# A graph kernel's adjacency, cast and turned by DMA instead of by TensorE, with maxima over two segments at once

## The reference

```python
# layer 0: maximum over the neighbours, 0 for a row without any
masked = jnp.where(mask[:, :, None], x[None, :, :], neg)
out = jnp.where(has_nbr[:, None], jnp.max(masked, axis=1), 0)
x = _layernorm(x + out)
# layer 1: attention over the neighbours
h = x @ W
e = leaky_relu((h @ a_src)[:, None] + (h @ a_dst)[None, :], 0.2)
att = softmax(jnp.where(valid, e, -1e9), axis=1)         # valid: adj > 0
attention = jnp.where(att >= 1e-4, att, 0) * L[:, None]  # L: neighbours of the row
x = _layernorm(x + elu(h + attention @ h))
```

## Time and profile before

| | us |
|---|---|
| median of 3 runs | 1084.57 (1081.44 to 1092.72) |
| the profiled execution, its own time | 1078.43 |
| its span | 1076.5 |
| PE, DVE, ACT, POOL busy | 779.5, 675.2, 609.9, 272.1 |
| DMA | 169.08 MB, mean 157 GB/s |

### The profile page before, as it was taken

One profiled execution on the slowest core, in us unless ns is written; L12 is line 12 of the kernel. 1 busy time (PEld: TensorE's weight loads), 2 busy tenths in 40 slices (PEclk: granted clock), 3 DMA queues, 4 the chain that ended last, 5 costly groups with the idle time before them and its releaser, 6 DMA issues.

```text
span 1076.5 us, 16405 instructions
## 1 busy us (share of the span) xinstructions
PE 779.5 (72%) x5872; PEld 595.6 (55%) x5935; DVE 675.2 (63%) x1662; ACT 609.9 (57%) x1257; POOL 272.1 (25%) x275
## 2 busy tenths in 40 slices
PE   1698976957968959659779320399989899998615
PEld 0365644634635636436446120298889888888314
DVE  6558577557666766656675812648667766865371
ACT  1886663834835726526537100557977977885413
POOL 7100732713705607407417274000000000000000
PEclk9999998989979989979989655599999999999757
DMA  9287796894985976956977525531442354151200
GB/s 331 88 268 238 218 187 209 232 210 137 268 208 157 235 209 194 187 188 203 195 235 189 49 67 30 182 122 35 173 168 73 123 181 143 40 181 36 90 0 5
DMA packets 69154, 169.08 MB, mean 157 GB/s; under 512 B 7311, under 2 KB 27920, under 8 KB 68912
## 3 DMA queue, kind: packets, MB, share of 16 engines
q1 hardware_dynamic: 60672, 148.98, 40.4%
q0 software_dynamic: 8400, 19.02, 16.3%
HBM read 129.11 MB, written 40.96 MB: 158 GB/s over the span
## 4 chain that ended last, share of the span: by engine, by line
PE 42%; DVE 27%; DMA 13%; issue 9%; ACT 6%; POOL 3%; DVEq 0%; POOLq 0%
DMA adj_in<-in_adj_dram 12%; PE psS L900 11%; PE psT L1049 7%; DVE adj_in L1490 7%; PE psT L875 7%; PE psR L1049 6%; ACT adj_in L768 3%; PE psR L884 2%; DVE acc L1227 2%; POOL G L621 1%; DVE ident L1171 1%; DVE wide L1327 1%; PE psR L1115 1%; DVE listed L1323 1%; PE psS L945 1%
## 5 line engine op out<-in xcount | busy, mean ns | idle before, releaser
L684 ACT ACTIVATE at<-psT 126x512 bf16<-126x512 int32 (+1 forms) x264 | 157.4, 597 | 222.3 <-PE psT L875 221.7
L1227 DVE TENSOR_TENSOR acc<-acc,psS 128x512 f32<-128x512 f32 x248 | 168.9, 684 | 170.9 <-PE psS L900 170.2
L900 PE MATMUL psS<-hot,x_split 128*128 128x512 bf16 x774 | 224.0, 395 | 39.9 <-DVE acc L1227 23.6
L875 PE MATMUL psT<-ident,adj_in 128*126 128x128 f32 (+1 forms) x1056 | 177.0, 293 | 44.2 <-DMA adj_in<-in_adj_dram 44.2
L621 POOL DMA_INDIRECT G<-x_tab_dram,idx x128 | 121.3, 948 | 334.5 <-DVE y L1390 231.6
L1490 DVE SCALAR_TENSOR_TENSOR adj_in<-adj_in,at 128x3072 f32<-128x3072 f32 (+1 forms) x48 | 148.3, 3090 | 70.6 <-ACT adj_in L768 70.6
L768 ACT ACTIVATE adj_in<-acc,minus,r_col 128x512 f32<-128x512 f32 x264 | 189.3, 803 | 2.5 <-PE psT L1049 2.5
L692 ACT ACTIVATE hot<-psR 128x512 bf16<-128x512 f32 x264 | 156.3, 592 | 0.2 <-PE psR L884 0.2
L875 PEld LDWEIGHTS psT<-ident,adj_in 128*126 128x126 f32 (+1 forms) x1056 | 121.5, 148 | 50.2 <-DMA adj_in<-in_adj_dram 44.7
L1049 PE MATMUL psT<-h_seg,adj_in 128*128 128x130 f32 x1056 | 126.3, 281 | 21.0 <-DVE adj_in L1490 20.6
L900 PEld LDWEIGHTS psS<-hot,x_split 128*128 128x128 bf16 x792 | 75.5, 100 | 118.8 <-DVE acc L1227 32.1
(11 more groups left out here) (272 smaller groups left out, 876.9 us busy)
## 6 DMA issues: line engine op xcount, KB each, us to landing
adj_in<-in_adj_dram SPq DMA_DIRECT2D x24, 1512.0 KB, 14.3
adj_in<-in_adj_dram SPq DMA_DIRECT2D x16, 1260.0 KB, 7.2
adjT_dram<-at SPq DMA_DIRECT2D x24, 768.0 KB
at<-adjT_dram SPq DMA_DIRECT2D x24, 768.0 KB, 7.9
adjT_dram<-at SPq DMA_DIRECT2D x24, 640.0 KB
at<-adjT_dram SPq DMA_DIRECT2D x24, 640.0 KB, 5.3
adj_in<-in_adj_dram SPq DMA_DIRECT2D x8, 1136.0 KB, 7.1
own<-in_x_dram SPq DMA_DIRECT2D x8, 256.0 KB
```

Of the source, the lines that this page charges most:

```text
L684: nc.scalar.activation(at[0:w, s, :], psT[0:w, n % 2, :].bitcast(I32), ACT.Sign).then_inc(at_ready, 1)
L875: mm = nc.tensor.transpose(psT[0:w, n % 2, t * P:(t + 1) * P], adj_in[:, q % ADJ_RING, t, (s - s0) * SEG:(s - s0) * SEG + w].bitcast(F32), ...
L900: mm = nc.tensor.matmul(psS[:, b, :], x_split[:, k, s, :], hot[:, n % 3, :], start=(k == 0), stop=(k == 2))
L1227: V.tensor_tensor(acc[:, b, :], acc[:, b, :], psS[:, b, :], ALU.max).then_inc(free[b], 1)
```

## The change

- GpSimd's queue casts `adj` into a bf16 tensor in DRAM, `adj_bf` (row pitch 4096 + 256 elements): six column parts for group 0, then four DMAs of 128 rows for each group. Groups 1 and 2 follow at once, group g + 3 between the gathers of group g.
- SP turns part by part from `adj_bf` into `at`, which now has two buffers of a group, by DMAs with `transpose=True`. The part of group g + 2 waits for the codes and squares of group g. The transposes on TensorE, the evictions on ACT, the ring `adj_in`, the stores to `adjT` and their reloads are gone; the attention stage turns its parts from `adj_bf` again.
- ACT squares two segments at once with a sum, which checks that the entries are 0 or 1.
- 32 segments of 128, of which 127 columns are fetched by `select` and the last is always listed; the markers in partitions 126 and 127 become a bias on ACT and one small matmul a part into the code bank. Ten blocks of 15 codes (9 of 14 before), ten extras (12 before).
- psS has two buffers of 1024 columns; psT lies in their second halves. A pair of segments fills one buffer, and DVE takes one maximum over 1024. `hot` has four buffers, was three.
- The late steps have new places, counted in pairs. `make_lists` comes ahead of `extra_rows`; the gather waits for `direct_max` (`direct_read`), not for `aggregate`; its fifth row has a place in G and not in gmax. The two `heads` are one.
- At the start x is loaded in three pieces, DVE blanks its last partitions, the large memset on POOL is gone, and the three splits of x run part by part in a pipeline.

```diff
+PITCH = N + 256
+AHEAD = 3
@@ sync
-            def load_adj(q):
-                    sp.wait_ge(turned, before_q // NPARTS * SEGS + PARTS[before_q % NPARTS][1])
-                sp.dma_start(adj_in[:, q % ADJ_RING, :, 0:c1 - c0], adj_g[g][:, :, c0:c1]
-            def store_part(q):
-                sp.wait_ge(at_ready, g * SEGS + PARTS[k][1])
-                sp.dma_start(adjT[g][:, PARTS[k][0]:PARTS[k][1], :], at_part(k)).then_inc(at_stored, 16)
+            def turn_part(q):
+                s0, s1 = PARTS[k]
+                if g == 0:
+                    sp.wait_ge(cast_part[k], 16)
+                else:
+                    sp.wait_ge(cast_group[g - 1], 16 * GT)
+                if g >= 2:
+                    sp.wait_ge(coded, (g - 2) * NPARTS + k + 1)
+                    sp.wait_ge(squared, (g - 2) * PAIRS + (s1 + 1) // 2)
+                sp.dma_start(at[:, g % 2, s0:s1, :], adj_bf[g * ROWS:(g + 1) * ROWS, s0 * SEG:s1 * SEG], transpose=True
+                             ).then_inc(turned[g % 2][k], 16)
...
             for g in range(GROUPS + 2):
                 for k in range(NPARTS):
+                    if g + 2 < GROUPS:
+                        turn_part((g + 2) * NPARTS + k)
+                    if k == 5 and g >= 2:
                         store_x1(g - 2)
...
-                sp.dma_start(at_ring[q % 5][:, 0:s1 - s0, :], adjT[g][:, s0:s1, :]).then_inc(at_loaded[q % 5], 16)
+                sp.dma_start(at_ring[q % 5][:, 0:s1 - s0, :], adj_bf[g * ROWS:(g + 1) * ROWS, s0 * SEG:s1 * SEG],
+                             transpose=True).then_inc(at_loaded[q % 5], 16)
@@ gpsimd
-            pool.memset(at[96:P, 0:SEGS - 1, :], 1.0).then_inc(consts_pool, 1)
+            def cast_tile(g, t):
+                row = g * ROWS + t * P
+                pool.dma_start(adj_bf[row:row + P, 0:N], adj[row:row + P, :]).then_inc(cast_group[g - 1], 16)
+
+            for k, (s0, s1) in enumerate(PARTS):
+                pool.dma_start(adj_bf[0:ROWS, s0 * SEG:s1 * SEG], adj[0:ROWS, s0 * SEG:s1 * SEG]).then_inc(cast_part[k], 16)
...
+            for g in range(1, AHEAD):
+                for t in range(GT):
+                    cast_tile(g, t)
             def gather_direct(g):
                 pool.wait_ge(list_ready, g + 1)
                 if g:
-                    wait_taken(pool, "acc_turn", g - 1)
+                    pool.wait_ge(direct_read, g)
...
+                    if t % 2 and g + AHEAD < GROUPS:
+                        cast_tile(g + AHEAD, t // 2)
             def gather_extra(g):
...
+                    if k % 5 == 4 and g + AHEAD < GROUPS:
+                        cast_tile(g + AHEAD, 2 + k // 5)
@@ scalar
-                nc.scalar.activation(at[0:w, s, :], psT[0:w, n % 2, :].bitcast(I32), ACT.Sign).then_inc(at_ready, 1)
+            def square(g, u):
+                for k in {PART_OF[2 * u], PART_OF[2 * u + 1]}:
+                    act.wait_ge(turned[g % 2][k], 16 * (g // 2 + 1))
+                if g * PAIRS + u:
+                    act.wait_ge(squared, g * PAIRS + u)
+                nc.scalar.activation(squares[:, :].rearrange("p (s i) -> p s i", s=2), at[:, g % 2, 2 * u:2 * u + 2, :],
+                                     ACT.Square, accum_out=square_sums[:, g * PAIRS + u:g * PAIRS + u + 1]
+                                     ).then_inc(squared, 1)
@@ tensor
-                for t in range(GT):
-                    mm = nc.tensor.transpose(psT[0:w, n % 2, t * P:(t + 1) * P],
+                if s == PARTS[k][0]:
+                    pe.wait_ge(turned[g % 2][k], 16 * (g // 2 + 1))
...
+                    nc.tensor.matmul(psC[:, q % 2, 0:GT * m * CODES], two_ones[0:2, :],
+                                     code_row[0:2, s0:s1, :].rearrange("p s c -> p (s c)").unsqueeze(1)
+                                     .to_broadcast([2, GT, m * CODES]), start=True, stop=False, skip_group_check=True)
@@ vector
-                    V.tensor_tensor(acc[:, b, :], acc[:, b, :], psS[:, b, :], ALU.max).then_inc(free[b], 1)
+                    V.tensor_tensor(acc_flat, acc_flat, psS[:, b, :], ALU.max).then_inc(free[b], 1)
```

More of the change, by code:

```diff
@@ L84, in fills @@
     for g in range(GROUPS + 2):
-        for s in range(SEGS):
+        for u in range(PAIRS):
             if g < GROUPS:
-                order.append(("select", g, s))
+                order.append(("select", g, u))
             for what, at, later in LATE:
-                if s == at and 0 <= g - later < GROUPS:
+                if u == at and 0 <= g - later < GROUPS:
                     order.append((what, g - later, 0))
@@ L316, in build @@
         split_low = sem("split_low")
-        h_blank = sem("h_blank")
-        adj_loaded = [sem(f"adj_loaded{b}") for b in range(ADJ_RING)]
-        turned = sem("turned")
-        at_ready = sem("at_ready")
-        at_stored = sem("at_stored")
+        cast_part = [sem(f"cast_part{k}") for k in range(NPARTS)]
+        cast_group = [sem(f"cast_group{g}") for g in range(1, GROUPS)]
+        turned = [[sem(f"turned{b}_{k}") for k in range(NPARTS)] for b in range(2)]
+        squared = sem("squared")
+        direct_read = sem("direct_read")
         ranked = sem("ranked")
@@ L494, in _ @@
                 sp.dma_start(a3[:, 2:3], a[0:D, :]).then_inc(weights_loaded, 16)
-            load_adj(2)
+            for q in range(NPARTS):
+                turn_part(q)
             sp.dma_start(x_tab[1:N + 1, :], x).then_inc(tab_stored, 16)
@@ L754, in spread_rho @@
                     act.wait_ge(relu_ready, (g - 1) * SEGS)
-                nc.scalar.activation(rho[:, g % 2, :], psS[:, 0, :], ACT.Exp, bias=cols[:, 3:4], scale=1.0 - ALPHA
+                nc.scalar.activation(rho[:, g % 2, :], psS[:, 0, 0:ROWS], ACT.Exp, bias=cols[:, 3:4], scale=1.0 - ALPHA
                                      ).then_inc(rho_ready, 1)
@@ L762, in relu_part @@
                     act.wait_ge(w_used, q - 2)
+                elif q == 0:
+                    act.wait_ge(coded, GROUPS * NPARTS)
+                    i = FILL["select", GROUPS - 1, PAIRS - 1]
+                    act.wait_ge(filled[i % 2], i // 2 + 1)
+                    act.wait_ge(squared, GROUPS * PAIRS)
                 if k == 0:
@@ L959, in x1_turn, with heads @@
                 mm.then_inc(filled[b], 1)
-            def heads(g, i):
-                b = claim((f"heads{i}", g, 0))
+            def heads(g):
+                b = claim(("heads", g, 0))
                 wait_taken(pe, "x1_turn", g)
-                for j, s in enumerate(H_PARTS[g][i]):
-                    w = width(s)
-                    mm = nc.tensor.matmul(psS[0:w, b, j * HPAD:j * HPAD + HCOLS], x1T[:, s * SEG:s * SEG + w],
+                for t in range(GT):
+                    at_col = t // 2 * 512 + t % 2 * HPAD
+                    mm = nc.tensor.matmul(psS[:, b, at_col:at_col + HCOLS], x1T[:, (g * GT + t) * P:(g * GT + t + 1) * P],
                                           w_aug[:, :], start=True, stop=True)
@@ new lines, in split_off @@
+            def split_off(k, i):
+                s0, s1 = PARTS[k]
+                dve.wait_ge((split_high, split_mid)[i], k + 1)
+                V.tensor_tensor(xs[:, s0:s1, :], xs[:, s0:s1, :], x_split[:, i, s0:s1, :], ALU.subtract
+                                ).then_inc((split_rest, split_rest2)[i], 1)
+            for k in range(NPARTS + 1):
+                for i in range(2):
+                    if 0 <= k - i < NPARTS:
+                        split_off(k - i, i)
+            acc_flat = acc[:, :, :].rearrange("p b i -> p (b i)")
@@ L1223, in best @@
+            merge_mark = [0]
+            last_max = [None]
+            def best(g, u):
+                b = wait_fill(dve, ("select", g, u))
+                if u == 0:
                     if g:
                         after(merge_mark[0])
-                    V.tensor_copy(acc[:, b, :], psS[:, b, :]).then_inc(free[b], 1)
+                    V.tensor_copy(acc_flat, psS[:, b, :]).then_inc(free[b], 1)
                 else:
-                    V.tensor_tensor(acc[:, b, :], acc[:, b, :], psS[:, b, :], ALU.max).then_inc(free[b], 1)
@@ L1228, in best @@
-                last_max[b] = FILL["select", g, s] // 2 + 1
-            merge_mark = [0]
+                    dve.wait_ge(free[last_max[0][0]], last_max[0][1])
+                    V.tensor_tensor(acc_flat, acc_flat, psS[:, b, :], ALU.max).then_inc(free[b], 1)
+                last_max[0] = (b, FILL["select", g, u] // 2 + 1)
             def join(g):
-                for b in range(2):
-                    dve.wait_ge(free[b], last_max[b])
+                dve.wait_ge(free[last_max[0][0]], last_max[0][1])
```

481 lines of the change are left out of this document (204 added, 277 removed).

## The result

The changed kernel took 1122.8 us in the median of four runs (1100.37 to 1161.7), the kernel before 1085.91 on the same chip. Two of the four executions (1138.04 and 1161.7) are much longer than the others, and the ratio leaves them out. It is 1.0188, with a 95% interval of 1.0128 to 1.0247: slower by 1.3 to 2.5%, where 1005 us was forecast. In a later series the ratio came to 1.0067 (0.9996 to 1.0138), which by itself could not be told from no change. The profiled execution took 1100.37 us, with a span of 1098.3.

A forecast was written before the change was run, and what follows sets the result against it. Selection was taken as bound by DMA with half a group's look-ahead, and still DMA-bound but better packed afterwards. 1078.4 - 59 (selection) - 9 (lists, gathers) - 8 (attention) = 1002; 1005 us was predicted for the median, range 905 to 1120.

The forecast's parts named there:

- Startup nothing: Start of selection: DMA work exceeds the engines' own end of 454 us, so an earlier first select gains nothing.
- Engines alone 54 us a group: Selection after the change: VectorE 48 us busy, with waits some 54 a group; by engines alone selection ends at 454.
- -59: Selection: last select at 540 us against 599.4, from DMA work of 530 plus 9 for the last part.
- 28.27 us piece of the chain: Selection before, chain of waits at 208.20 us: an adjacency load, read as DMA holding selection; five groups had one over 20.
- C + T = 44: DMA work of a group in selection: casts 28 us plus transposing reads 16 us.
- Doubled psS buffers let DVE fall a pair behind, so its lists stall PE less: Selection: VectorE may lag TensorE by a pair, not a segment, so its lists stall TensorE less; no separate size.
- Rival A: Every turned part, both passes: transposes cost what small pieces cost, slower; break-even 26 us a group, about 1235 at 41; chance 0.25.
- Rival C: TensorE without transposes falls to 1.2 GHz: 73 us a group with late steps, no selection gain, 1061 us; chance 0.06.
- B: Casts and transposes in selection run at the plain rate, 24.4 + 12.2 us a group: 916 to 942 us; chance 0.20.
- D: Transposes and casts together take about 53 us a group: selection ends where it did, within 1% in all; chance 0.07.
- Queues: POOL's and SP's queues: casts between gathers just covered; x1 store and own-rows load behind transposes have half a group to spare.
- -9 and -8 forecast: After selection: -9 us from earlier decode and lists and two fewer gathers; -8 from 32 instead of 33 attention segments.

The follow-up runs named there:

- the phases: No kernel: only DMAs of one group's 512 rows, in twelve phases, each kind alone or together; casts 22 us, turned parts 23.5, both at once 42.

## Why the prediction was wrong

**The step that failed** is the sum of the DMA engines as the bound of selection, and the two statements that let it stand: that by engines alone selection would end at 454 us, and that therefore "the startup is worth nothing in the forecast". Selection closed at 641.7, not at 540: a late first part costs 48.2 us, and the steady groups, forecast 60 to 66 us apart, stayed at 74.8 because TensorE, VectorE and ScalarE wait for each other at the late steps (59.1 us without casts and with these steps moved).

1. *Startup nothing*: measured +48.2, the largest term of the whole change. I had counted DMA work as a sum that could be packed in any order. The first turned part needs about one sixth of a group's cast; it landed only when all 12.6 MB of the fourteen casts were through, 8.4 MB of them for groups 1 and 2. The last 10 us of that wait, at 20 GB/s with next to no casts left, stay unexplained. Holding back casts took the first close to between 86 and 101 us in every version that had it.
2. *Engines alone 54 us a group*: measured 69.7 (before, loads quartered), 73.2 (changed, no casts) and 59.1 (the same with the late steps moved). I had taken VectorE's 48 busy plus six for waits, from a window whose idle time I blamed on DMA. With the loads cut, TensorE is busy 57 of 68 us; with the casts gone it is busy 49 of 71 and waits. Of the -59 forecast the groups after the first gave -5.9. The reading of the earlier trace rows was right so far that DMA was a bound, worth 56 us in that run. It was wrong in taking the 28.27 us piece of the chain for lost time, where TensorE stood 44.2 us in all of selection, and in that a second bound stood right under the first.
3. *C + T = 44*: confirmed in size, 22 + 23.5 = 45.5, though C was taken too dear (28) and T too cheap (16). What the sum leaves out is who is served first. The gathers' 22 us a group look too dear: 20 gathers alone, of consecutive rows, took a share of 0.18 of 26.6 us, which is 4.8 us, and I had taken their price from a trace in which other transfers ran beside them. With about 7 for 30 gathers and 45.5 for C and T the same sum would be some 446 us, an estimate, far below the 641.7 measured. The DMA share over selection does add up to 0.83 x 642 = 533 us, but the share goes over 1 at 20 GB/s (80 to 84 us above), so it is not work alone, and its nearness to 530 confirms nothing. The page "DMA: Bandwidth & Descriptors" of the Trainium skill (Latency and other measured facts) gives 261 GB/s for such a transpose, from which 16 us was an estimate. The runs do not agree: 4.2 MB took 23.5 us alone, 179 GB/s, with SP spending about 3.5 us on the issue of each part.
4. *Doubled psS buffers let DVE fall a pair behind, so its lists stall PE less*: wrong. TensorE's wait for `has_extra` ahead of prefix was 2.5 us in all before, once; in the changed kernel it is 49.3 us, in all eight groups, and ScalarE's wait for `mv` went from one to eight. These waits are new, and the version with moved late steps is rid of the first (16.0, once). That each late step now takes a buffer from a whole pair is my explanation; it was not tested by itself.
5. *Rival A* had the right sign and the wrong mechanism: the parts cost 23.5 us a group, under its break-even of 26, and are slow only behind casts. *Rival C* was given 0.06 because a slow TensorE is a busy TensorE; the clock did fall, to 0.80 in steady groups, and its price of 73 us a group is near the 74.8 measured. But TensorE is busy in only 52 of 76 us, so it is not the bound that C describes. The clock is part of the 14.1 us a group between the two versions without casts; its share was not separated. Nothing speaks for *B* or *D*. The 1309 ns for a block by the crossbar (the Trainium skill, page "VectorE: DVE Perf Modes", The three transpose paths) would be an estimated 168 us for a group one after another. The runs show 23.5, so it is no price for a stream.
6. *Queues*: "behind them stand the store of x1 and the load of own rows, which have half a group to spare" was the right place and the wrong verdict. Half a group is not enough where the issue of one part takes 59 us, and the one longer execution of the changed kernel that was traced lost its 60 us in such a group.
7. *Right*: the Square at 1.05 us against 1.06, the maximum at 1.217 against 1.22; the Relu with its bias took 0.685, dearer than the 0.592 assumed (that it is the bias was not tested). What follows selection: -9 and -8 forecast, -20.5 measured. The attention stage's reloads stayed hidden.

## What to carry to other kernels

A sum of DMA work is a bound only if what is needed first is also served first: bulk transfers that run ahead must be held back until the small ones that an engine waits for have landed, at the start above all. Before a gain is booked to the removal of one bound, the suspect has to be priced by the time that an engine stands for it (here 44.2 us, not five pieces of over 20), and the next bound has to be read as a time between events, not as busy time plus a guess. Taking the suspect away (here, three quarters of the loads) prices it in one run. And a step that is free under one bound, as the order of the late steps was, is worth trying again once that bound is gone: 97 us here.

## What the runs showed of the hardware

A transposing DMA of 256-byte packets and a converting DMA of up to 7-KB packets share the engines by packets rather than by bytes: 0.28 MB against 3.65 MB in 20 us, 1111 packets against 494. With plain loads of 2.7-KB packets it was 2707 against 2944. Apart from that, shares near or over 1 at 20 to 60 GB/s appeared in the kernels when both were in flight, and not in the phases by themselves. Gathers and turned parts together cost no more than the gathers. And the same kernel took 1086 to 1100 us in four series and 1271 to 1275 in two. The trace of its quartered version from one of these two has 220.9 us of waits on VectorE alone that no event in the trace ends; their cause is not known.
